# Values by head group with the first group moved into the image before, and a reordered opening of image 0, in a fused vision-transformer layer

## The chip, the cores and the metric

The kernel runs on one core of a Trainium2 chip. The metric is device time in microseconds (us) of one execution, taken as the median of several runs. The engines are PE (TensorE: matmuls, transposes, weight loads), DVE (VectorE), ACT (ScalarE), POOL (GpSimd) and SP (SyncE, which only issues transfers here). All run their own instruction streams in order and meet at semaphores.

## The reference

Eight images of 3 x 512 x 512 are cut into 1024 patches of 768 values each and go through one transformer layer with a mixture-of-experts feed-forward part. What matters here:

```
h = patches @ Wp + bp + (relu(xy @ W1 + b1) @ W2 + b2)       # 1024 x 256 for each image
a = layernorm(h)                                             # no gamma, beta
n = layernorm(a) * gamma + beta
q, k, v = split(n @ W_qkv.T)                                 # 8 heads of 32
gate = sigmoid(a @ W_gate.T + b_gate)
attn = softmax(q k^T / sqrt(32))                             # 1024 x 1024 for each head
out = (attn^T v) * gate                                      # weights indexed by query i, summed over i
h = h + a + out @ W_final.T + b_final
x = layernorm(h)
H = gelu(x @ W1 + b1);  probs = softmax(H @ Wg + bg)         # 1024 hidden, 8 experts
h = h + probs[argmax] * (H @ Wd[argmax] + bd[argmax])
```

All is float32 in and out.

## The kernel before

**Tiles.** An image is 1024 tokens, 8 tiles of 128 rows by 256 columns. `hres` holds h for two images in turn, `a` the first norm, `n` the second; `nt` and `at` are n (with gamma and beta) and a, transposed. `qk` holds q and k of one head group in a high and a low part, each [32 rows per head, 1024], and `stq`, `stk` hold these stacked three times in 96 rows (high/high, low/high, high/low), so that one matmul gives scores of full precision. `v` is [128, 8 tiles, 256], `vs` is v divided by the softmax sums, `pr` a ring of eight tiles of exponentials. PSUM (`ps`) has 8 banks of 512 columns: 0 to 3 take scores of two steps in turn, 4 and 5 the attention output, 6 and 7 (`spare`) everything else.

**Loops.** For each image b there are 64 steps k: two head groups of 32 steps (`G_STEPS`), each step one head and one tile of 128 queries. A step is `score` (PE, two matmuls of 512 columns), a maximum (DVE, `nmax`), an exponential with its sum (ACT), and, every fourth step, `scale_v` (DVE) and then `weigh` (PE). Score k waits for exponential k - 2. All else is put between the steps by hand-written tables (`QK1_AT`, `EMBED_AT`, `GATE_AT`, `TURN_AT`, `QK0_AT`, and `LOW*_AT`, `WEIGH_AT`). While image b runs its steps, PE also projects q and k of group 1 (steps 0 to 7), embeds image b + 1 (steps 8 to 31), and in the second half computes gates, transposes n and a of image b + 1 and projects q and k of its group 0 (steps 49 to 59). Step 32 holds the long insertion: `router(b - 1)` on PE and ACT (the hidden layer and the logits of the image before), and on DVE `norm_1(b + 1)` (statistics and a), `block_turn` (32 x 32 transposes of the hidden layer for the store), `stats_2`, the logit copies and `norm_2` (n). POOL computes each norm's reciprocal root (`root`: one addition, one power) and adds a and the final bias into `hres`.

**The seam between images.** After step 63 PE runs `values(b, 0)`, the last `weigh` of the image before, `values(b, 1)`, `final(b - 1)`, the gates of group 0 and then score 0. ACT reads v out of PSUM, DVE applies the gate, adds the result of `final` into `hres` and takes the statistics of the third norm. SP issues the 24 stacking transfers of group 0 once all scores of the image before are done, and score 0 waits for all 24.

**The opening.** PE computes the position term of all tiles first (K=3 matmul, relu, K=128 matmul, and a K=2 matmul that adds the bias), ACT copies it to `posb`, then PE embeds image 0 tile by tile through two buffers (`xt`), which SP refills. DVE and ACT, which split w_ffn1 into two parts, and PE wait for all 20 constants (`consts`) first. Then DVE and POOL do both norms, PE transposes and projects, and image 0 starts. After image 7 a router, a sort of all tokens by expert and the expert matmuls follow; nothing there is touched.

On PE the lines of the trace are: L430, L437 and L438 position, L448 embedding, L460 transposes of n and a, L469 q and k, L481 scores, L495 `weigh`, L509 values, L515 gates, L531 `final`, L544 transposes for the router, L552 to L554 hidden layer, L562 and L569 logits. On DVE L873 and L877 are statistics, L883 normalises, L910 makes the low part of q or k, L891 adds the embedding, L967 is `block_turn`, L1020 the maximum; on SP L287 and L289 are the stacking transfers.

## Time and profile before

| | |
|---|---|
| median of 3 runs | 1888.89 us (1886.69 to 1890.84) |
| the profiled execution | 1891.02 us, its span 1889.2 us |
| busy: PE, DVE, ACT, POOL | 1668.8, 1222.3, 946.8, 311.1 us |
| busy share of the span | 88%, 65%, 50%, 16% |
| first score | 114.27 us |
| first values matmul of images 0, 1, 2, 3 | 96.53, 254.27, 425.73, 599.02 us |
| stacking transfers | 2 x 192 of 128 KB, median 2.5 us from issue to landing |
| DMA, mean over the span; highest slice | 99 GB/s; 206 GB/s |

All times are from the start of the span. "Busy" of PE adds up overlapping instructions' stretches once; matmul ends are modelled. A row of the timeline merges neighbouring instructions of one kind. Its numbers are the start, the length, the engine, the line, what is written and read, the shape, the count, and in brackets the engine's idle time before it with what ended that. An fp32 matmul of the program is two PE instructions in the trace (x24 is 12 matmuls); a transpose is one.

### The profile page before, as it was taken

Reading aid. Unit: us, or ns where it says so; the run is one execution under the profiler, and the core shown is the slowest. Engines: PE = TensorE matmul, PEld = TensorE weight load, DVE = VectorE, ACT = ScalarE, POOL = GpSimd, SP = SyncE. Lnnn points to the kernel's source line nnn. Section 1 sums busy time; section 2 is a strip of 40 time slices with the busy share of each in tenths; the row PEclk is TensorE's granted clock in tenths of the full one; section 3 lists DMA queues with packets and bytes.
Section 4 is the critical chain, followed back from the end, with each engine's and each line's share of the span. In section 5 each row is a group of like instructions: output and inputs, shape, how many; then the busy total and the mean of one; then the engine's idle time right before and its main releaser. Section 6 shows DMA issues by size and latency. Waiting matters only on the chain.

```text
span 1889.2 us, 29246 instructions
## 1 busy us (share of the span) xinstructions
PE 1668.8 (88%) x10884; PEld 1128.4 (60%) x10884; DVE 1222.3 (65%) x2027; ACT 946.8 (50%) x1564; POOL 311.1 (16%) x239
## 2 busy tenths in 40 slices
PE   8587799989999999999899999999797715999998
PEld 4445456646655564566466555645353504999998
DVE  0347767776776887677767768776766487444443
ACT  1144656575665657565746656475655330222222
POOL 0200200200020011002000200200000072455553
PEclk9789899999999999999999999999898957999999
DMA  3133041704342252417044432513060391566663
GB/s 117 34 92 95 15 106 51 156 1 116 96 101 62 79 129 46 107 51 156 4 121 100 91 83 65 129 38 90 11 146 1 85 205 62 181 202 206 205 198 133
DMA packets 124151, 187.31 MB, mean 99 GB/s; under 512 B 14941, under 2 KB 89325, under 8 KB 123888
## 3 DMA queue, kind: packets, MB, share of 16 engines
q1 hardware_dynamic: 108016, 121.48, 27.5%
q0 software_dynamic: 16000, 63.98, 10.4%
q8 instruction: 91, 1.49, 0.3%
q14 instruction: 44, 0.36, 0.1%
HBM read 84.72 MB, written 51.38 MB: 72 GB/s over the span
## 4 chain that ended last, share of the span: by engine, by line
PE 66%; DVE 19%; issue 7%; ACT 4%; DMA 1%; POOL 1%; SPq 1%; POOLq 0%; DVEq 0%; ACTq 0%
PE ps L481 12%; PE ps L722 11%; PE ps L495 10%; PE ps L448 8%; DVE nmax L1020 6%; PE ps L469 3%; PE ps L710 3%; DVE bst L873 3%; ACT pr L819 3%; PE ps L531 3%; PE ps L509 3%; PE ps L552 2%; PE ps L554 2%; PE ps L553 2%; PE ps L515 2%
## 5 line engine op out<-in xcount | busy, mean ns | idle before, releaser
L1020 DVE TENSOR_REDUCE nmax<-ps 128x1 f32<-128x1024 f32 x512 | 624.0, 1221 | 228.4 <-PE ps L481 219.5
L819 ACT ACTIVATE pr<-ps,nmax 128x1024 f32<-128x1024 f32 x512 | 570.1, 1114 | 302.5 <-DVE nmax L1020 297.6
L481 PE MATMUL ps<-stk,stq 96*128 96x512 f32 x1024 | 411.5, 486 | 78.2 <-ACT pr L819 57.9
L481 PEld LDWEIGHTS ps<-stk,stq 96*128 96x128 f32 x1024 | 171.6, 195 | 278.8 <-ACT pr L819 167.1
L495 PE MATMUL ps<-pr,vs 128*32 128x256 f32 x4096 | 275.1, 390 | 16.2 <-DVE vs L922 16.2
L722 PE MATMUL ps<-wd,hg 128*128 x1728 | 225.4, 287 | 0.0
L343 POOL TENSOR_SCALAR vare<-mv 128x8 f32<-128x8 f32 x24 | 5.7, 238 | 1311.2 <-DVE mv L877 1311.2
L722 PEld LDWEIGHTS ps<-wd,hg 128*128 128x128 f32 x1728 | 212.7, 193 | 0.0
L495 PEld LDWEIGHTS ps<-pr,vs 128*32 128x32 f32 x4096 | 109.8, 110 | 165.5 <-issue 78.5
L853 ACT ACTIVATE hg<-ps 128x512 fp32r<-128x512 f32 x144 | 78.5, 597 | 240.6 <-PE ps L710 240.6
L448 PE MATMUL ps<-wp,xt 128*128 128x256 f32 x768 | 196.1, 382 | 2.2 <-DMA xt<-x_in 1.5
L448 PEld LDWEIGHTS ps<-wp,xt 128*128 128x128 f32 x768 | 145.5, 190 | 31.7 <-DMA xt<-x_in 2.7
L789 ACT ACTIVATE ht<-ps,bf 128x512 f32<-128x512 f32 x128 | 88.0, 688 | 139.9 <-PE ps L554 138.3
L469 PE MATMUL ps<-nt,wqk 128*128 128x512 f32 x256 | 133.0, 605 | 3.5 <-DVE qk L910 2.8
L1141 DVE TENSOR_TENSOR hg<-ps,hg 128x512 fp32r<-128x512 f32 x144 | 92.9, 685 | 49.6 <-ACT hg L853 49.5
L552 PE MATMUL ps<-nt_high,wf 128*128 128x512 f32 x256 | 105.3, 411 | 1.8 <-DVE nt_low L959 1.5
L1148 DVE SCALAR_TENSOR_TENSOR rows<-ps,slot_prob,rows 128x256 f32<-128x256 f32 x72 | 34.8, 483 | 111.0 <-PE ps L724 111.0
L554 PE MATMUL ps<-nt_high,wf 128*128 128x512 f32 x256 | 103.7, 405 | 0.0
L553 PE MATMUL ps<-nt_low,wf 128*128 128x512 f32 x256 | 102.6, 401 | 0.0
L819 ACT ACTIVATION_READ_ACCUMULATOR pr<-ps,nmax 128x1 f32 x512 | 99.5, 194 | 0.0
L408 POOL DMA_INDIRECT out<-rows,slot_to x72 | 72.3, 1004 | 125.0 <-DVE rows L1148 115.0
L710 PE MATMUL ps<-ident,rows 128*128 128x128 f32 x576 | 76.3, 277 | 7.2 <-DMA rows<-token_rows,slot_from 7.2
(122 smaller groups left out, 1811.0 us busy)
## 6 DMA issues: line engine op xcount, KB each, us to landing
xt<-x_in SPq DMA_DIRECT2D x64, 384.0 KB, 3.1
stq<-qk SPq DMA_DIRECT2D x192, 128.0 KB, 2.5
stk<-qk SPq DMA_DIRECT2D x192, 128.0 KB, 2.5
token_rows<-staged_b SPq DMA_DIRECT2D x64, 256.0 KB, 4.2
token_rows<-staged_a SPq DMA_DIRECT2D x64, 256.0 KB, 4.5
token_rows<-hres POOLq DMA_DIRECT2D x8, 1024.0 KB, 5.2
wd_raw<-w_down SPq DMA_DIRECT2D x64, 128.0 KB, 3.3
rows<-token_rows,slot_from POOLq DMA_INDIRECT x72, 4.7
```

Source lines behind the costliest of these rows:

```text
L448: last = mm(spare(t)[:, 0:D], xt[:, t % 2, k, :], wp[:, k, :], start=(k == 0), stop=(k == KC - 1))
L469: last = mm(spare(j), wqk[:, c, w * D + g * P:w * D + (g + 1) * P], nt[:, c, hf * HALF:(hf + 1) * HALF], start=(c == 0), stop=(c == DC - 1))
L481: last = mm(ps[:, 2 * (k % SR) + j, :], stq[:, hh, i * P:(i + 1) * P], stk[:, hh, j * 512:(j + 1) * 512], start=True, stop=True)
L495: last = mm(ps[32 * hh:32 * hh + 32, O_BANK + j // 2, (j % 2) * D:(j % 2 + 1) * D], vs[:, gi % 2, hh, :], pr[:, (4 * gi + hh) % PR, j * D: ...
L552: mm(spare(bank), w_high, nt_high[:, c, half], start=(c == 0), stop=False)
L553: mm(spare(bank), w_high, nt_low[:, c, half], start=False, stop=False)
L554: last = mm(spare(bank), w_low, nt_high[:, c, half], start=False, stop=(c == DC - 1))
L710: last = nc.tensor.transpose(ps[:, 2 * (s % 2) + c, q * P:(q + 1) * P], rows[:, s % RING, (4 * c + q) * P:(4 * c + q + 1) * P], ident[:])
L722: mm(o, hg[:, s % 2, h_part, k, :], wd[:, w_part, bass.ds(e, 1), k, :], start=(k == 0 and h_part == w_part), stop=False)
L819: actv(pr[:, k % PR, :], ps[:, 2 * (k % SR):2 * (k % SR) + 2, :].rearrange("p a n -> p (a n)"), ACT.Exp, bias=nmax[:, k % 16:k % 16 + 1], ...
L1020: V.reduce_max(nmax[:, k % 16:k % 16 + 1], ps[:, 2 * (k % SR):2 * (k % SR) + 2, :].rearrange("p a n -> p (a n)"), AX_X, negate=True).then_ ...
L1141: V.tensor_tensor(hg[:, s % 2, 1, 4 * c:4 * c + 4, :].rearrange("p k n -> p (k n)"), ps[:, 2 * (s % 2) + c, :], high_part.bitcast(F32), AL ...
```

## The change

1. **Values by head group.** `values(b, g, h)` computes the 128 columns of head group g for four tiles. It is 8 matmuls of 128 columns; before, a block was 4 matmuls of 256 columns. Group 0 of image b + 1 is computed in steps 61 and 63 of image b (`VALUE_AT`), and read by ACT there (`valued`); group 1 stays at the seam.
2. **Opening.** SP loads x of image 0 ahead of the constants, six tiles of it into the ring `pr`; w_patch, pos_w2 and the bias are issued by ACT, the bias broadcast to all partitions. PE embeds four tiles while ACT applies the relu, then alternates two position tiles with one embedding tile. The position term's bias is added by DVE. DVE takes each tile's statistics between the additions. The wait for the constants is split in two (`early`, `consts`), and the split of w_ffn1, now staged in the second half of `hres`, comes after the first values.
3. **One set of statistics for both norms.** With variance s of h, a's variance is s / (s + eps), so 1 / sqrt of (s + eps) and of (s (1 + eps) + eps^2) normalise h directly to a and to n. `stats_2` and one call of `root` go for each image. POOL does two additions and one power of 16 elements (before, twice one addition and a power of 8). n is normalised before a, both after the logit copies; the transposes of n and a wait for each separately; POOL's sum waits for a.
4. **Stacking.** One transfer moves the q and the k part of a row block: 12 of 256 KB for a group instead of 24 of 128 KB, with a semaphore for each head, and each of the first four scores waits for its head's three.

The diff, cut to its core:

```diff
+        st = tensor(sa, "st", [96, 2, 4, TOKENS], F32R)
+        stq, stk = st[:, 0], st[:, 1]
...
+        STACK = ((0, 3, 2), (1, 3, 1), (0, 4, 3))
...
+        VALUE_AT = {G_STEPS + 29: 0, G_STEPS + 31: 1}
...
+            for dst, src in ((posin, pos_in), (posw1, pos_w1)):
+                sp.dma_start(dst, src).then_inc(S["pos_in0"], 16)
+            for t in range(2):
+                sp.dma_start(xt[:, t], x[0, t]).then_inc(x_in[t], 16)
+            for t in range(2, TILES):
+                sp.dma_start(x_first[:, t - 2], x[0, t]).then_inc(S[f"x_first{t // 2 - 1}"], 16)
+            for dst, src in ((vecs[:, 0, :], ln_gamma), (vecs[:, 1, :], ln_beta), (vecs[:, 2, :], b_gate),
+                             (ident[:], identity), (wqk[:], w_qk), (wv[:], w_v), (wg[:], w_gate)):
+                sp.dma_start(dst, src).then_inc(S["early"], 16)
+            for dst, src in ((bfin[:], b_final), (wf1_in, w_ffn1), (wfin[:], w_final), (bf1[:], b_ffn1),
...
-                    for r in range(3):
-                        src = slice(32 * hh, 32 * hh + 32)
-                        dst = slice(32 * r, 32 * r + 32)
-                        sp.dma_start(stq[dst, hh, :].bitcast(F32), qk[src, 0, r % 2, :].bitcast(F32)
-                                     ).then_inc(stacked[g], 16)
-                        sp.dma_start(stk[dst, hh, :].bitcast(F32), qk[src, 1, r // 2, :].bitcast(F32)
-                                     ).then_inc(stacked[g], 16)
+                    src = slice(32 * hh, 32 * hh + 32)
+                    for r, (first, end, step) in enumerate(STACK):
+                        sp.dma_start(st[32 * r:32 * r + 32, :, hh, :].bitcast(F32),
+                                     qk_parts[src, first:end:step, :].bitcast(F32)).then_inc(stacked[g][hh], 16)
...
+            def root_1(b):
+
+                hold(pool, "var1", b + 1)
+                nc.gpsimd.tensor_scalar(vare[:, 0], mv[:, 0, :, 1], EPS, None, ALU.add).then_inc(S["eps1"], 1)
+                nc.gpsimd.tensor_scalar(vare[:, 1], mv[:, 0, :, 1], 1.0 + EPS, EPS * EPS, ALU.mult, ALU.add
+                                        ).then_inc(S["eps1"], 1)
+                wait(pool, "eps1", 2 * b + 2)
+                nc.gpsimd.tensor_tensor(rstd[:, 0:2], vare[:, 0:2], half_neg[:], ALU.pow).then_inc(S["rstd1"], 1)
...
+            def position(t):
+                o = ps[:, 4 + t // 2, (t % 2) * D:(t % 2 + 1) * D]
+                for c in range(DC):
+                    last = mm(o, posr[:, c, t * P:(t + 1) * P], posw2[:, c, :], start=(c == 0), stop=(c == DC - 1),
+                              skip_group_check=True)
+                last.then_inc(S["pos_mm2"], 1)
+
+            def first_embed(t):
+                if t < 2:
+                    wait(pe, x_in[t], 16)
+                elif t % 2 == 0:
+                    wait(pe, f"x_first{t // 2 - 1}", 32)
+                source = xt[:, t] if t < 2 else x_first[:, t - 2]
+                for k in range(KC):
+                    last = mm(ps[:, t // 2, (t % 2) * D:(t % 2 + 1) * D], source[:, k, :], wp[:, k, :],
+                              start=(k == 0), stop=(k == KC - 1), skip_group_check=True)
+                last.then_inc(S["emb_mm"], 1)
+
+            pe.wait_ge(S["pos_in0"], 16 * 2)
             for c in range(DC):
                 for hf in range(2):
-                    mm(ps[:, 2 * c + hf, :], posw1[:, c * P:(c + 1) * P], posin[:, hf * HALF:(hf + 1) * HALF],
+                    mm(ps[:, 4 + 2 * c + hf, :], posw1[:, c * P:(c + 1) * P], posin[:, hf * HALF:(hf + 1) * HALF],
                        start=True, stop=True).then_inc(S["pos_mm"], 1)
+            pe.wait_ge(S["wp_in"], 16)
+            for t in range(4):
+                first_embed(t)
+            pe.wait_ge(S["pos_in1"], 16 * 2)
             pe.wait_ge(S["pos_relu"], 4)
-            pe.wait_ge(S["setup"], 1)
-            for t in range(TILES):
-                o = ps[:, 4 + t // 2, (t % 2) * D:(t % 2 + 1) * D]
-                for c in range(DC):
-                    mm(o, posr[:, c, t * P:(t + 1) * P], posw2[:, c, :], start=(c == 0), stop=False, skip_group_check=True)
-                mm(o, ones[0:2, :].bitcast(F32), posbias, start=False, stop=True, skip_group_check=True).then_inc(S["pos_mm2"], 1)
-            pe.wait_ge(S["pos_done"], 4)
+            for t in range(4):
+                position(2 * t)
+                position(2 * t + 1)
+                first_embed(t + 4)
...
-                wait(pe, "n_ready", b + 1)
+                wait(pe, ("n_ready", "a_ready")[w // 2], b + 1)
...
-                if k % G_STEPS == 0:
-                    wait(pe, stacked[g], (b * 24 + 24) * 16)
+                if k % G_STEPS < 4:
+                    wait(pe, stacked[g][hh], (b + 1) * 3 * 16)
...
-            def values(b, pair):
-                if pair == 0:
-                    wait(pe, "qk_lo", b * 8 + 4)
-                for j in (2 * pair, 2 * pair + 1):
-                    if j >= 2:
-                        wait(pe, "v_read", b * 4 + j - 1)
-                    for t in range(2):
-                        for c in range(DC):
-                            last = mm(spare(j)[:, t * D:(t + 1) * D], nt[:, c, (2 * j + t) * P:(2 * j + t + 1) * P],
-                                      wv[:, c, :], start=(c == 0), stop=(c == DC - 1), skip_group_check=True)
-                    last.then_inc(S["v_mm"], 1)
+            def values(b, g, h):
+                if g == 0:
+                    wait(pe, "qk_lo", b * 8 + 3 + h)
+                else:
+                    wait(pe, "v_read", b * 4 + h + 1)
+                for t in range(4):
+                    for c in range(DC):
+                        last = mm(spare(h)[:, t * P:(t + 1) * P], nt[:, c, (4 * h + t) * P:(4 * h + t + 1) * P],
+                                  wv[:, c, g * P:(g + 1) * P], start=(c == 0), stop=(c == DC - 1),
+                                  skip_group_check=True)
+                last.then_inc(S["v_mm"], 1)
...
-                for t in range(TILES):
-                    for part in range(3):
-                        embed(b, t, part)
-                wait(pe, "emb_h", b * TILES + TILES)
+                wait(pe, "pos_done", 4)
                 for j in range(8):
                     turn(b, j)
                 wait(pe, "tr_read", b * 8 + 8)
                 for j in range(4):
                     for c in range(DC):
                         project(b, 0, j, c)
+                for h in range(2):
+                    values(b, 0, h)
+            pe.wait_ge(S["early"], 16 * N_EARLY)
+            front_start(0)
             pe.wait_ge(S["consts"], 16 * N_CONSTS)
-            front_start(0)
...
-                values(b, 0)
+                values(b, 1, 0)
                 if before:
                     for j in range(4):
                         weigh(b - 1, 15, j)
-                values(b, 1)
+                values(b, 1, 1)
...
+                    if after and k in VALUE_AT:
+                        values(b + 1, 0, VALUE_AT[k])
...
+            nc.scalar.dma_start(wp[:], w_patch).then_inc(S["wp_in"], 16)
+            nc.scalar.dma_start(posw2, pos_w2).then_inc(S["pos_in1"], 16)
+            nc.scalar.dma_start(posbias, pos_bias[None, :, :].broadcast_to([P, 2, D])).then_inc(S["pos_in1"], 16)
...
+            def valued(b, g, h):
+                wait(act, "v_mm", b * 4 + 2 * g + h + 1)
+                wait(act, "vs_ready", b * 16 - 8 * (1 - g))
+                actv(v[:, 4 * h:4 * h + 4, g * P:(g + 1) * P], spare(h).rearrange("p (t d) -> p t d", t=4), ACT.Identity,
+                     scale=0.5).then_inc(S["v_read"], 1)
...
-            def stats_2(b):
-                wait(dve, "a_ready", b + 1)
-                stats(a, b, 2)
-            def norm_2(b, before):
+            def norm_2(b, par, before):
                 if before:
                     wait(dve, "xt_mm", b * 4 - 4)
-                normalise(n, a, b, 2, "n_ready")
+                normalise(n, hres[:, par], b, 2, "n_ready")
+                normalise(a, hres[:, par], b, 1, "a_ready")
...
+                if t % 2 == 0:
+                    wait(dve, "pos_mm2", t + 2)
+                    V.tensor_tensor(posb[:, t:t + 2, :], ps[:, 4 + t // 2, :].rearrange("p (t d) -> p t d", t=2),
+                                    posbias[:, 0, None, :].broadcast_to([P, 2, D]), ALU.add).then_inc(S["pos_done"], 1)
+                    wait(dve, "pos_done", t // 2 + 1)
                 embedded(0, 0, t)
-            norm_1(0, 0)
-            stats_2(0)
-            norm_2(0, False)
+                if t >= 1:
+                    wait(dve, "emb_h", t)
+                    V.bn_stats(bst[:, 0, t - 1, :], hres[:, 0, t - 1, :])
+            wait(dve, "emb_h", TILES)
+            V.bn_stats(bst[:, 0, TILES - 1, :], hres[:, 0, TILES - 1, :]).then_inc(S["stats1"], 1)
+            aggregate(0, 1)
+            norm_2(0, 0, False)
             for j in range(4):
                 low(0, 0, j)
+            dve.wait_ge(S["wf1_high"], 1)
+            V.tensor_tensor(wf1[:, 1], wf1_in, wf1[:, 0].bitcast(F32), ALU.subtract).then_inc(S["setup"], 1)
...
-                        if after:
-                            stats_2(b + 1)
...
-                            norm_2(b + 1, before)
+                            norm_2(b + 1, 1 - par, before)
```

**PE, the opening** (after the branch, before that of the first rows; `wp` is w_patch, `pr` after the change also holds x):

```order
L437 MATMUL ps<-at,nt 128x256 x2
L438 MATMUL ps<-at,ones 128x256
L448 MATMUL ps<-wp,xt 128x256 x48
L460 MATMUL ps<-ident,n 128x128 x8
```

That was before, where the first two rows stand eight times. Now:

```order
L450 MATMUL ps<-wp,xt 128x256 x12
L450 MATMUL ps<-wp,pr 128x256 x12
L439 MATMUL ps<-at,nt 128x256 x4
L450 MATMUL ps<-wp,pr 128x256 x6
L439 MATMUL ps<-at,nt 128x256 x4
```

The K=2 matmuls (L438) are gone; half of the embedding stands first, and the other half alternates with the position tiles.

**PE, from step 61 of image 0 to score 0 of image 1**, before:

```order
L481 MATMUL ps<-stk,stq 128x512 x4
L495 MATMUL ps<-pr,vs 32x256 x8
L481 MATMUL ps<-stk,stq 128x512 x4
L495 MATMUL ps<-pr,vs 32x256 x8
L509 MATMUL ps<-wv,nt 128x256 x8
L495 MATMUL ps<-pr,vs 32x256 x16
L509 MATMUL ps<-wv,nt 128x256 x8
L531 MATMUL ps<-wfin,gate 128x256 x16
```

and now:

```order
L509 MATMUL ps<-st 128x512 x4
L536 MATMUL ps<-wv,nt 128x128 x8
L523 MATMUL ps<-pr,vs 32x256 x8
L509 MATMUL ps<-st 128x512 x4
L536 MATMUL ps<-wv,nt 128x128 x8
L523 MATMUL ps<-pr,vs 32x256 x8
L536 MATMUL ps<-wv,nt 128x128 x8
L523 MATMUL ps<-pr,vs 32x256 x16
L536 MATMUL ps<-wv,nt 128x128 x8
L559 MATMUL ps<-wfin,gate 128x256 x16
```

Two of four blocks of values now stand between score 61 and score 62, and behind score 63, each ahead of a `weigh`.

**DVE, at step 32 of image 1**, before:

```order
L873 BN_STATS bst<-hres 128x6 x8
L877 BN_AGGR mv<-bst 128x2 x8
L883 TENSOR_SCALAR a<-hres,mv,rstd 128x256 x8
L967 STREAM_TRANSPOSE staged_b<-ht 128x16x32 x4
L873 BN_STATS bst<-a 128x6 x8
L877 BN_AGGR mv<-bst 128x2 x8
L967 STREAM_TRANSPOSE staged_a<-ht 128x16x32 x4
L974 COPY xt<-ps 128x512
L978 COPY logits<-ps 128x32
L883 TENSOR_SCALAR n<-a,mv,rstd 128x256 x8
```

and now:

```order
L908 BN_STATS bst<-hres 128x6 x8
L915 BN_AGGR mv<-bst 128x2 x8
L1002 STREAM_TRANSPOSE staged_b<-ht 128x16x32 x4
L1002 STREAM_TRANSPOSE staged_a<-ht 128x16x32 x4
L1009 COPY xt<-ps 128x512
L1013 COPY logits<-ps 128x32
L921 TENSOR_SCALAR n<-hres,mv,rstd 128x256 x8
L921 TENSOR_SCALAR a<-hres,mv,rstd 128x256 x8
```

The second statistics are gone and a has moved behind the logit copies.

## Rows read from the trace of the kernel before

**Rows 1.** The page, the chain of work that ended last, share by engine.

```profile
PE 66%; DVE 19%; issue 7%; ACT 4%; DMA 1%; POOL 1%; SPq 1%; POOLq 0%; DVEq 0%; ACTq 0%
```

**Rows 2.** Timeline, opening (start, length, engine, what, count, idle before).

```profile
4.24 7.19 PE L430 MATMUL ps<-pr 3*128 3x512 f32 x8 [4.24 <-DMA at<-pos_bias]
...
12.12 2.08 PE L437 MATMUL ps<-at,nt 128*128 128x256 f32 x4 [0.69 <-ACT nt L742]
...
38.10 6.90 PE L448 MATMUL ps<-wp,xt 128*128 128x256 f32 x24 [0.69 <-ACT posb L745]
39.96 2.29 DVE L868 TENSOR_TENSOR wf<-a,wf 128x2048 fp32r<-128x2048 f32 x1 [24.13 <-ACT wf L749]
...
57.38 5.45 PE L448 MATMUL ps<-wp,xt 128*128 128x256 f32 x24 [0.53 <-DMA xt<-x_in]
```

**Rows 3.** Busy us by stretch: PE, PEld, DVE, ACT, POOL, granted clock, DMA, GB/s.

```profile
12.00:38.00 26.00, 25.30 (x48) 13.39 (x48) 0.17 (x1) 2.40 (x6) 0.00 (x0) 1.00 0.16 52
...
528.00:540.00 12.00, 12.00 (x47) 9.58 (x47) 8.67 (x18) 4.47 (x7) 8.86 (x2) 0.86 0.69 138
701.00:713.00 12.00, 12.00 (x59) 9.15 (x62) 9.38 (x20) 5.72 (x8) 8.57 (x2) 1.00 0.77 152
```

**Rows 4.** Timeline, the norms of image 0 and the transposes.

```profile
66.07 0.64 DVE L877 BATCH_NORM_AGGREGATE mv<-bst 128x2 f32<-128x6 f32 x8
66.89 0.24 POOL L343 TENSOR_SCALAR vare<-mv 128x8 f32<-128x8 f32 x1 [66.04 <-DVE mv L877]
67.23 1.67 POOL L346 TENSOR_TENSOR rstd<-vare,half_neg 128x8 f32<-128x8 f32 x1
...
77.15 2.67 DVE L883 TENSOR_SCALAR n<-a,mv,rstd 128x256 f32<-128x256 f32 x8 [2.12 <-POOL rstd L346]
...
82.02 1.94 PE L460 MATMUL ps<-ident,a 128*128 128x128 f32 x8
```

**Rows 5.** Timeline, from the last low part to the first score.

```profile
95.78 0.69 DVE L910 SCALAR_TENSOR_TENSOR qk<-ps,qk 128x512 fp32r<-128x512 f32 x1 [1.03 <-ACT qk L769]
...
96.53 7.17 PE L509 MATMUL ps<-wv,nt 128*128 128x256 f32 x32 [1.41 <-DVE qk L910]
...
103.54 3.60 PE L515 MATMUL ps<-at,wg 128*128 128x512 f32 x8
...
111.51 0.59 SPq L289 DMA_DIRECT2D stk<-qk  x1
...
114.27 1.22 PE L481 MATMUL ps<-stk,stq 96*128 96x512 f32 x2 [7.13 <-DMA stk<-qk]
```

**Rows 6.** Timeline of DVE, middle of image 0.

```profile
178.22 2.70 DVE L873 BATCH_NORM_STATS2 bst<-hres 128x6 f32<-128x256 f32 x8
...
195.71 2.35 DVE L1020 TENSOR_REDUCE nmax<-ps 128x1 f32<-128x1024 f32 x2
```

**Rows 7.** Timeline of PE, seam between images 2 and 3.

```profile
594.98 1.07 PE L495 MATMUL ps<-pr,vs 128*32 128x256 f32 x16 [0.65 <-DVE vs L922]
...
597.35 0.73 PE L481 MATMUL ps<-stk,stq 96*128 96x512 f32 x2 [0.64 <-ACT pr L819]
...
599.02 3.72 PE L509 MATMUL ps<-wv,nt 128*128 128x256 f32 x16
...
618.03 1.04 PE L481 MATMUL ps<-stk,stq 96*128 96x512 f32 x2
```

**Rows 8.** Timeline of DVE and PE, middle of image 2.

```profile
520.76 2.67 DVE L873 BATCH_NORM_STATS2 bst<-a 128x6 f32<-128x256 f32 x8
...
527.11 1.06 PE L569 MATMUL ps<-pick,xt 128*128 128x8 f32 x8 [0.95 <-DVE xt L974]
...
541.01 2.32 DVE L1020 TENSOR_REDUCE nmax<-ps 128x1 f32<-128x1024 f32 x2
```

**Rows 9.** Timeline of PE, transposes for the router in image 2.

```profile
506.54 1.97 PE L544 MATMUL ps<-ident,n 128*128 128x128 f32 x16
```

**Rows 10.** Line L509: length of one in ns, least, median, most.

```profile
L509 PEld LDWEIGHTS ps<-wv,nt x256: 185/190/191, 96.5 to 1297.2; 128*128 128x128 f32 x128
```

115 lines of the change are left out of this document (53 added, 62 removed).

## The prediction

> **What bounds the kernel now.** I read the chain of waits first: two thirds of it is PE, a fifth DVE [rows 1]. That share is a mean over stages, so I then read the timeline engine by engine for four places that the change touches: the opening of image 0, the middle of image 0 (step 32), the middle of a later image, and the seam between two images. What is to be seen:
>
> - Opening. PE computes the position term, then embeds, then waits 17 us for two layer norms, then projects, then waits for the stacking DMAs. The first score starts at 114.27 [rows 5]. PE is busy 25.30 of the 26 us from 12 to 38 and its granted clock is recorded as 1.00 [rows 3], yet four instructions of 256 columns take 2.08 us there, and in the last third of the embedding 24 of the same shape take 5.45 [rows 2]: 0.50 against 0.227 us each, the pace of 1.2 against 2.4 GHz. The change of pace lies inside the first 24 embedding instructions (6.90 us).
> - Middle of image 0. No router runs there, and DVE alone carries it: 178.22 to 195.71, from the statistics of image 1 to the first maximum of the second head group [rows 6].
> - Middle of a later image. PE idles 0.95 us before the small logit transposes, since DVE was late [rows 8].
> - Seam. From 599.02 PE runs without a gap to the first score at 618.03 [rows 7], and DVE goes from the statistics of the last layer norm straight into the first maximum. Before that, in the last three score steps, PE idles 0.65 us (waiting for the scaled v) and 0.64 us (waiting for the exponentials) [rows 7].
>
> From about 175 on the middle part of each image (steps 8 to 31) is PE throughout and is not touched; the tail after image 7 is not touched either.
>
> **The opening, term by term.** After the change PE starts once the first two small loads have landed. Before, it waited for four and started at 4.24; I take 3.6 (no more than 4.24 in any case). The 4 matmuls of K=3 keep their 7.19 us [rows 2]: 10.8. Then come 96 embedding instructions and 32 for the position term without the K=2 matmuls (those 8 leave PE). The first 12 embedding instructions, in which the pace changed, took 6.90 less 12 x 0.227, about 4.2 us; the other 116 at 0.227 take 26.3: PE ends at 41.3. If the position matmuls stay at 0.50, it is 32 x 0.27 = 8.7 more; if none of it ever gets fast, 128 x 0.50 = 64, so 75. I take the fast pace, since the same kind of instruction (128 rows, 256 columns) had it in the embedding [rows 2] and no K=2 matmul stands between them any more. The loads: w_patch, pos_w2 and the bias move to ACT's queue and x goes ahead of the constants. At the 384 KB of one x tile it is 4.3 MB in all by 25 us, when PE wants the last tiles, 172 GB/s, which the page's busy slices reach; so I cost the reordering at nothing; the cover is the 7.19 us of K=3 matmuls for w_patch, and a late w_patch costs its lateness one for one.
>
> DVE's per-tile statistics now run between the embeddings; the last two adds, two statistics and the 0.64 us of aggregation end 2.4 us after PE: 43.7, against 66.71 before [rows 4]. **Gain 23.0.**
>
> From there to n: before 66.71 to 79.82, 13.1 us (two rounds of statistics, POOL, normalise). After: two additions of 0.24 instead of one, one power, one normalise of 2.67 [rows 4]. The power now has 16 elements instead of 8; nothing in the trace shows that size. Bounds: 1.67 (no dearer) and 3.34 (twice); I take 3.3, because a row of 8 elements at 1.67 against an addition at 0.24 is work per element. 0.2 + 0.24 + 0.24 + 0.1 + 3.3 + 0.1 + 2.7 = 6.9. **Gain 6.2** (7.9 at the low bound). a is now normalised after n, and the third group of transposes, which began 2.2 us after n was done [rows 4], can begin 2.7 after: **loss 0.5.**
>
> From the last low part (ends 96.47) to the first score (114.27): 17.8 us, set by 24 issues on SP, the last at 111.51 and landing 2.7 later; PE's values and gates were done by 107.1 [rows 5]. Now the score needs the first 3 of 12 DMAs. Each carries twice the bytes. Bounds for one issue: 0.59 [rows 5] and 1.2 (twice). At the high bound the first three land 3.6 + 2.7 = 6.3 us in and the last of 12 at 17.1; the fourth score is wanted some 7 us after the first, at about 16.6, so even this costs half a microsecond, and at 0.59 nothing. PE becomes the limit: values begin 1.4 us before the last low part is done (PE waited that long for it [rows 5], and the first block now needs three parts only), then 7.6 us of values (a run is costed below) and 3.45 of gates: 9.7. **Gain 8.1.** The split of w_ffn1 moves in here, on ACT between two reads of v and on DVE before the first maximum (2.29 us [rows 2]), both while PE works on values and gates for 9.7 us; if that cover fails it costs what is left over, at most the 2.29.
>
> Opening in sum: 23.0 + 6.2 - 0.5 + 8.1 = 36.8, so the first score at about 77.5. PE no longer idles 7.13 us before it [rows 5], and the first scores then ran at half pace (1.22 us for what takes 0.73 later [rows 5, 7]): 1 us more. **37.8.**
>
> **Middle of image 0.** Of the 17.5 us between 178.22 and 195.71 [rows 6], the second statistics (2.71 + 0.64) and a POOL round of 2.1 us go, and 0.24 + 1.65 for the larger power come: **gain 3.5** (5.2 if the power costs 1.67). Score 32 wants its three DMAs at about 180, so what is late next is still DVE.
>
> **Middle of images 1 to 6.** Without the second statistics (2.67 + 0.64 [rows 8]) DVE follows the GELUs and has the logit sums before PE asks: the 0.95 us go, and with them about 0.3 of the wait in PE's queue. But n and a are now both normalised after this point, 2.67 us more on DVE before the turns of the second half. From the small transposes to the first maximum it was 13.90 us here [rows 8], with a mean clock of 0.86 over the twelve from 528 [rows 3]; that is 3.4 us at half, which costs 1.6. In the next image the same stretch has 1.00 (the row from 701), so some 12.3; I take the two to alternate. Laid end to end DVE now needs 1.3 + 5.35 + 1.2 + 8 x 0.6 = 12.7 us from there. So the gain is 1.25 where PE's dip stays, and 0.8 where DVE becomes the limit; both bounds: 0 and 2.1 (dip gone). **6 x 1.0 = 6.0.** Image 7 normalises nothing, gain 0.
>
> **Seam, seven times.** All of v for one image is 32 PE instructions of 256 columns in two runs of 3.72 us [rows 7]. After: four runs of 16 instructions of 128 columns. Nearest rows for such a run: 16 transposes with 128 columns and a full weight load, 1.97 us to the end of the last [rows 9]; 8 instructions with full fp32 weight loads and hardly any columns, 1.06 us [rows 8], or 0.13 each. So 1.9 a run: v costs what it cost. Two runs leave the seam (3.7 us) and enter steps 61 and 63, where PE idled 1.29 us, which is all they can hide in. Going through the steps: score 62 starts 1.2 us later, score 63 0.5 later, the last weighing and final each 1.2 earlier. ACT's two reads of 0.6 us stand behind exponentials 61 and 63 while ACT waits for DVE anyway. As final moves, so do DVE's adds, statistics and the first maximum. Bounds 0.3 and 1.4; **7 x 1.2 = 8.4.** The 12 stacking DMAs have some 23 us there, from the end of score 63 to the fourth score of the next image (618.03 and some 4 us more), so they cost nothing up to 1.7 us each.
>
> The Trainium skill speaks against this cut. Its page "TensorE: Matmul & The Clock Gate", section "Back-to-back issue gap", says that with a weight load for each matmul the spacing at 128 columns is above what the columns alone give (about 81 ns instead of 56). As an estimate from that page, 1.45 times the half of 0.227 would be 0.165 us an instruction, and the sum about 24 us worse. Rows 8 and 9 show 0.12 to 0.13, and I go by them.
>
> **Sum.** 37.8 + 3.5 + 6.0 + 8.4 = 55.7. The profiled execution took 1891.02 us, so 1835.3; it was 2.13 us over the median of the runs shown, so 1833.2 in their terms.
>
> **Rivals.**
> 1. The slow clock stays. PE was busy from 12 to 38 and still at the 1.2 GHz pace [rows 2, 3], so position and embedding together may not wake it. Against it: the embedding did. If all of it is slow, PE ends at 75 instead of 41.3: 34 us of the opening's gain are lost, 1867. (The Trainium skill, same page, section "What's actually happening", has sustained activity release the clock; the stretch from 12 to 38 does not agree with it as it stands.)
> 2. Only the opening pays. The seam and the later middles give nothing, because PE's filled idle time pushes the last scores and the exponentials by as much, and DVE's later n and a take the rest: 14.4 less, 1848.
> 3. Weight loads surface at 128 columns. A load of this kind is 0.19 us long [rows 10]; if the loads set the pace with their full length, a run costs 3.05, which is 1.15 more, four times in eight images: 37, so 1870. Against it: the 1.06 and the 1.97 us [rows 8, 9].
> 4. Slower: the merged stacking DMA is much dearer to issue. It reads two strided rows per partition into a strided tile; no row shows that form. Per DMA of c us, each seam loses 12 (c - 1.7) and the opening 12 (c - 1.16); the 55.7 us are gone at c = 2.2. At 2.4, four times today's 0.59, it is 74 us: 1907.
> 5. Better than summed: the power costs no more than now in both places (3.4), and the dips go: 1826.
> That the change doesn't do what it says is excluded by the order of the instructions.
>
> **How the numbers follow.** Forecast 0.55 (1833, own range 1824 to 1844, the upper end being the slow position matmuls), rival 1 0.12, rival 2 0.15, rival 3 0.06, rival 4 0.03, rival 5 0.07, near zero for some reason unseen 0.02. The range must reach rivals 2 and 5 and may leave out 1, 3 and 4, 0.21 in all: 1822 to 1850. Within 0.2% (3.8 us, what can be told from no change here) 0.01; slower 0.03; faster 0.96.
>
> **What would show it.** In the changed profile: first score near 77.5; embedding and position instructions at 0.227 us from about 15 on; the power at 3.3; step 32 of image 0 about 14 us after its first statistics; no PE idle time before the small transposes of images 1 to 6; runs of values of 1.9 us; final 1.2 us nearer to score 61. Wrong would be a pace of 0.50 beyond 20 us, values over 2.2 us a run, an issue above 1.2 us, or DVE later than PE at the seam for another reason than the statistics.

## The result and the profile after

The changed kernel takes 1824.16 us (median of 4 runs, 1823.65 to 1824.39) against 1889.07 us for the kernel before beside it (4 runs, 1886.69 to 1890.84): ratio 0.9657, 95% interval 0.964 to 0.9674. That is 64.9 us gained; 55.7 were forecast. The result lies within the forecast's range of 1822 to 1850, 9 us below its 1833. The profiled execution took 1824.39 us, 66.6 less than that of before, and the account below is made against that.

Lines have moved: L450 and L476 embed, L439 is the position term, L509 scores, L523 weighs, L536 computes values, L559 is the final projection, L597 the small logit transposes, L1066 the maximum, L296 the stacking DMAs.

The chain of work that ended last, and busy time of each engine; the chain has hardly changed in kind against [rows 1]:

```profile
PE 1631.2 (90%) x11124; PEld 1125.0 (62%) x11124; DVE 1201.0 (66%) x1904; ACT 943.0 (52%) x1560; POOL 307.8 (17%) x231
...
PE 68%; DVE 18%; issue 7%; ACT 5%; DMA 1%; SPq 1%; POOL 0%; POOLq 0%; DVEq 0%; ACTq 0%
```

The timeline of the opening, to be laid beside [rows 2, 4, 5] (start, length, engine, what, count, idle before it):

```profile
5.30 7.19 PE L457 MATMUL ps<-pr 3*128 3x512 f32 x8 [5.30 <-DMA pr<-pos_w]
12.42 8.13 PE L450 MATMUL ps<-wp,xt 128*128 128x256 f32 x24
20.39 5.34 PE L450 MATMUL ps<-wp,pr 128*128 128x256 f32 x24
25.57 1.89 PE L439 MATMUL ps<-at,nt 128*128 128x256 f32 x8
...
44.88 0.64 DVE L915 BATCH_NORM_AGGREGATE mv<-bst 128x2 f32<-128x6 f32 x8
...
46.35 2.94 POOL L350 TENSOR_TENSOR rstd<-vare,half_neg 128x16 f32<-128x16 f32 x1
...
49.32 2.67 DVE L921 TENSOR_SCALAR n<-hres,mv,rstd 128x256 f32<-128x256 f32 x8 [3.80 <-POOL rstd L350]
...
54.63 1.97 PE L488 MATMUL ps<-ident,a 128*128 128x128 f32 x8 [0.55 <-DVE a L921]
...
67.71 7.31 PE L536 MATMUL ps<-wv,nt 128*128 128x128 f32 x64
...
69.26 14.15 SPq L296 DMA_DIRECT2D st<-qk  x12
...
77.89 1.04 PE L509 MATMUL ps<-st 96*128 96x512 f32 x2
...
83.21 0.73 PE L509 MATMUL ps<-st 96*128 96x512 f32 x2 [2.09 <-DMA st<-qk]
...
87.28 1.22 PE L509 MATMUL ps<-st 96*128 96x512 f32 x2 [2.48 <-DMA st<-qk]
...
87.34 0.60 ACT L797 ACTIVATE qk<-ps 128x512 fp32r<-128x512 f32 x1 [4.57 <-DMA st<-qk]
```

What is to be seen: the first score starts at 77.89, against 114.27 before [rows 5] and 77.5 forecast. Then two scores wait 2.09 and 2.48 us for a stacking DMA each, and ACT waits 4.57 us for the last of them before it overwrites qk. The last score of the fence took 1.22 us instead of 0.73: PE came out of the wait at half its pace, as it had in [rows 5].

The values by line: length of one in ns (least, median, most), of the matmuls and of their weight loads:

```profile
L536 PE MATMUL ps<-wv,nt x512: 272/275/377, 67.7 to 1236.3; 128*128 128x128 f32 x171
...
L536 PEld LDWEIGHTS ps<-wv,nt x512: 186/192/193, 67.6 to 1236.2; 128*128 128x128 f32 x171
```

The page's row on the stacking DMAs (KB each, us from issue to landing):

```profile
st<-qk SPq DMA_DIRECT2D x192, 256.0 KB, 5.1
```

The seam between images 2 and 3, against [rows 7]:

```profile
549.98 0.73 PE L509 MATMUL ps<-st 96*128 96x512 f32 x2 [0.35 <-ACT pr L854]
...
550.54 1.95 PE L536 MATMUL ps<-wv,nt 128*128 128x128 f32 x16
...
552.42 1.07 PE L523 MATMUL ps<-pr,vs 128*32 128x256 f32 x16
...
554.46 1.95 PE L536 MATMUL ps<-wv,nt 128*128 128x128 f32 x16
...
563.07 7.07 PE L559 MATMUL ps<-wfin,gate 128*128 128x256 f32 x32
```

And three stretches as busy us of PE, PEld, DVE, ACT, POOL, granted clock, DMA share, GB/s: of image 1 from the router's transposes to the maximum of step 32 (the "middle"), then from there to its final projection, and the latter again for image 2 (the "second half"):

```profile
297.51:329.31 31.80, 30.99 (x184) 22.93 (x184) 23.83 (x59) 15.73 (x24) 9.22 (x5) 1.00 0.73 171
...
329.31:393.70 64.39, 59.52 (x460) 32.92 (x453) 45.73 (x57) 47.27 (x82) 3.35 (x1) 1.00 0.22 51
...
497.34:563.07 65.73, 60.89 (x460) 33.74 (x453) 45.82 (x57) 47.39 (x82) 3.35 (x1) 0.97 0.21 50
```

The same two second halves before, images 1 and 2:

```profile
367.98:434.80 66.82, 60.86 (x429) 32.18 (x421) 45.81 (x57) 47.54 (x82) 0.92 (x1) 0.97 0.20 44
...
541.01:608.09 67.08, 61.08 (x429) 32.12 (x421) 45.91 (x57) 47.65 (x82) 0.00 (x0) 0.97 0.21 44
```

The last four show what the forecast had not looked at. A second half comes in two lengths, 64.39 with a clock of 1.00 and about 65.73 with 0.97. Of images 0 to 6, all seven had a fall of the clock before; after, only images 0, 2 and 5 do. I cut both traces at the same events (a middle of image 0 runs from the first embedding of image 1 to the maximum of step 32); the account in us, before less after:

| part | forecast | measured | |
|---|---|---|---|
| opening, to the first embedding of image 1 | 37.8 | 31.6 | 131.23 to 99.60 |
| middle of image 0 | 3.5 | 4.1 | 64.48 to 60.37 |
| middles of images 1 to 6, at clock 1.00 | 6.0 | 6.8 | 32.94 to 31.80 |
| seven seams, at the same clock | 8.4 | 9.3 | 67.06 to 65.73 |
| clock falls that are gone, and image 7 and the tail | 0 | 14.7 | below |
| sum | 55.7 | 66.5 | 66.6 |

The 14.7: three middles of before, at a clock of 0.95, took 34.47 instead of 32.94, and no such fall is left (4.6); four second halves (images 1, 3, 4 and 6) lost theirs, at 1.3 or so each (5.2); image 7 gave 3.9 and the tail 1.5; the final-to-embedding stretches gave -0.4. Each trace is one execution. The opening of the changed kernel came to 99.60 in this one and to 98.15 in another below, and the opening of before, with the same instructions, to 131.23, 131.92 and 132.50, so this pair of traces gives the opening the least of what these would (31.6 to 34.4). Image 7 and the tail differ by as much among versions that don't touch them: the tail is 427.6 here, 429.2 in the run with 24 transfers and 429.6 in the one with the stacking by halves. Their 5.4 us can't be put down to the change.

### The profile page after: what moved, and what is told of

Its sections match the earlier page's. It is cut to its first block, busy times and chain, and to the rows that moved or that the text cites. A ratio compares the mean times of both kernels' runs of the same rounds, so it can differ in the third digit from the quotient of the medians.

```text
span 1822.6 us, 29454 instructions
## 1 busy us (share of the span) xinstructions
PE 1631.2 (90%) x11124; PEld 1125.0 (62%) x11124; DVE 1201.0 (66%) x1904; ACT 943.0 (52%) x1560; POOL 307.8 (17%) x231
## 4 chain that ended last, share of the span: by engine, by line
PE 68%; DVE 18%; issue 7%; ACT 5%; DMA 1%; SPq 1%; POOL 0%; POOLq 0%; DVEq 0%; ACTq 0%
PE ps L509 12%; PE ps L752 11%; PE ps L523 11%; PE ps L476 8%; DVE nmax L1066 6%; ACT pr L854 3%; PE ps L740 3%; PE ps L559 3%; PE ps L536 3%; PE ps L497 3%; PE ps L580 2%; PE ps L582 2%; PE ps L581 2%; PE ps L543 1%; PE ps L450 1%
## 5 line engine op out<-in xcount | busy, mean ns | idle before, releaser
L1066 DVE TENSOR_REDUCE nmax<-ps 128x1 f32<-128x1024 f32 x512 | 623.7, 1221 | 216.7 <-PE ps L509 209.8
L509 PE MATMUL ps<-st 96*128 96x512 f32 x1024 | 399.6, 474 | 70.5 <-ACT pr L854 60.8
L509 PEld LDWEIGHTS ps<-st 96*128 96x128 f32 x1024 | 168.2, 191 | 266.5 <-ACT pr L854 128.6
L523 PE MATMUL ps<-pr,vs 128*32 128x256 f32 x4096 | 271.7, 386 | 11.5 <-DVE vs L957 11.5
L523 PEld LDWEIGHTS ps<-pr,vs 128*32 128x32 f32 x4096 | 108.8, 109 | 153.4 <-issue 70.4
L476 PE MATMUL ps<-wp,xt 128*128 128x256 f32 x672 | 172.8, 378 | 0.0
L476 PEld LDWEIGHTS ps<-wp,xt 128*128 128x128 f32 x672 | 126.3, 189 | 25.2 <-DVE qk L945 1.2
```

What stands on the lines that cost most here:

```text
L476: last = mm(spare(t)[:, 0:D], xt[:, t % 2, k, :], wp[:, k, :], start=(k == 0), stop=(k == KC - 1))
L509: last = mm(ps[:, 2 * (k % SR) + j, :], stq[:, hh, i * P:(i + 1) * P], stk[:, hh, j * 512:(j + 1) * 512], start=True, stop=True)
L523: last = mm(ps[32 * hh:32 * hh + 32, O_BANK + j // 2, (j % 2) * D:(j % 2 + 1) * D], vs[:, gi % 2, hh, :], pr[:, (4 * gi + hh) % PR, j * D: ...
L1066: V.reduce_max(nmax[:, k % 16:k % 16 + 1], ps[:, 2 * (k % SR):2 * (k % SR) + 2, :].rearrange("p a n -> p (a n)"), AX_X, negate=True).then_ ...
```

## The experiments

Two things are to be explained: why the opening gave 6 us less than summed, and where 15 us came from that nobody had counted. My theory on the first is that the stacking DMAs are limited by the rate at which bytes move, with SP's issue time following from it; the rivals are the form of the merged DMA and SP's queue. On the second it is that short PE waits beside the small router matmuls let the clock fall; the rivals are that a term of the sum was simply worth more, or that something else shortened these stretches. The first four runs take the parts of the change back. "Beside it" is the kernel before, run on the same chip together with the changed one.

### The values back at the seam

```diff
-        VALUE_AT = {G_STEPS + 29: 0, G_STEPS + 31: 1}
+        VALUE_AT = {}
...
-                for h in range(2):
-                    values(b, 0, h)
...
-                values(b, 1, 0)
+                values(b, 0)
...
-                values(b, 1, 1)
+                values(b, 1)
```

values() and ACT's four reads of v are those of before.

> The changed kernel with the values as before the change: four blocks of 256 columns, all at the seam. Theory A (the seam gives 1.35 us for the move itself, and the rest of the 2.1 us a seam that the trace shows is PE's clock, which no longer falls): plus 7 x 1.35 = 9.5 us, 1833.6, and the clock falls as seldom as in the changed kernel. Theory B (the move gives all 2.1 us): plus 14.5, 1838.7.

Measured: 1835.13 us (1834.04 to 1837.48), beside it 1888.27; ratio 0.971 [0.9681, 0.9739]. So the cut of v is worth 11 us by the medians; the profiled execution, 1837.48, is the slowest of its four, and its span is 13.1 above that of the changed kernel. Image 2, middle's end to final:

```profile
500.95:568.01 67.06, 60.97 (x428) 32.25 (x421) 45.88 (x57) 47.58 (x82) 3.36 (x1) 0.97 0.23 54
```

The seven second halves of images 0 to 6 take 66.99 to 67.11 with a clock of 0.94 to 0.97; the middles stay at 31.78. Against 65.73 in the changed kernel, also with a fall, the move itself gives 1.33 a seam, 9.3 in all. The rest of the 13.1 is that four images got their fall back (4 x 1.35 = 5.4), and the short form of image 7's first half (66.43 against 67.60) gave 1.2 the other way. So theory A had the price of the move right, and its claim that the clock would fall as seldom as in the changed kernel was wrong. The fall comes some 5 us after step 32, where this kernel issues the same instructions as the changed one.

### Two statistics and two powers again

```diff
-                stats(hres[:, par], b, 1)
+                stats(hres[:, par], b, 1)
+                normalise(a, hres[:, par], b, 1, "a_ready")
...
+                        if after:
+                            stats_2(b + 1)
...
-                root_1(b)
+                root(1, b)
+                root(2, b)
```

n is normalised from a, as before; POOL does a power of 8 elements twice.

> The changed kernel with the second statistics and the second round of POOL put back, in the opening and for every image. Both theories: 6 us in the opening and 4 in the middle of image 0. For the six later middles theory A expects 1.15 us each and, because PE then idles 0.95 us again, the clock to fall again in some of them (1.5 us each time): 1841 to 1846. Theory B expects 1.15 us each and no change of the clock: 1841.

Measured: 1845.5 us (1841.52 to 1846.21), ratio 0.976 [0.9729, 0.979]: 21 us slower than the changed kernel. By place: opening 5.4, middle of image 0 4.1, middles of images 1 to 6 6.6 (32.90 against 31.80), the rest in the second halves (images 1 to 4 have a fall here, 2 and 5 in the changed kernel), image 7 and the tail. The middle of image 2, and in PE's timeline the small transposes in it:

```profile
477.18:510.08 32.90, 31.07 (x184) 22.81 (x184) 26.61 (x75) 15.73 (x24) 12.11 (x6) 1.00 0.79 183
```

```profile
497.76 1.06 PE L597 MATMUL ps<-pick,xt 128*128 128x8 f32 x8 [1.02 <-DVE xt L1013]
```

The 1.02 us of PE idle time before the small transposes is back, as in [rows 8], and so is the length of 32.9, but the clock stays at 1.00, where before three of six middles had 34.47. So the wait alone isn't enough for a fall, and its going is not shown to be why the middles lost theirs.

### Twenty-four stacking transfers

```diff
-                        sp.dma_start(st[32 * r:32 * r + 32, :, hh, :].bitcast(F32),
-                                     qk_parts[src, first:end:step, :].bitcast(F32)).then_inc(stacked[g][hh], 16)
+                        dst = slice(32 * r, 32 * r + 32)
+                        sp.dma_start(stq[dst, hh, :].bitcast(F32), qk[src, 0, r % 2, :].bitcast(F32)
+                                     ).then_inc(stacked[g][hh], 16)
+                        sp.dma_start(stk[dst, hh, :].bitcast(F32), qk[src, 1, r // 2, :].bitcast(F32)
+                                     ).then_inc(stacked[g][hh], 16)
```

> The changed kernel with the stacking as 24 transfers of 128 KB instead of 12 of 256 KB, still with a semaphore for each head. Theory A (the stacking is bound by bytes, some 170 GB/s): scores 1 to 3 of image 0 wait as long as now, 1824, within 1 us. Theory B (the merged form is what costs 1.18 us an issue and 5 us a landing): the waits of some 5 us go, 1819.

Measured: 1824.34 us (1822.97 to 1828.64), ratio 0.9658 [0.9625, 0.969]: no difference. The scores and ACT wait all the same:

```profile
85.72 1.22 PE L512 MATMUL ps<-st 96*128 96x512 f32 x2 [2.38 <-DMA st<-qk]
...
85.78 0.60 ACT L800 ACTIVATE qk<-ps 128x512 fp32r<-128x512 f32 x1 [4.05 <-DMA st<-qk]
```

SP issues 24 DMAs from 68.24 on, at 0.59 us and more each; the last issue begins at about 83.7. The 12 merged DMAs take 1.18 each to issue on the average (14.15 / 12) and land after 5.1, these cost half and land after 2.4. In the changed kernel the first three of the twelve were issued in 0.76, 0.59 and 0.75, with little under way, and the others in 1.11 to 1.40. So the merged form alone is no dearer to issue; the issue gets long once transfers are under way. The form of the DMA is not what the scores wait for. With 24 DMAs, 128 KB every 0.64 us is itself some 205 GB/s, so this run alone can't tell SP's own pace from a limit on the bytes; the 12 larger ones and the two queues below can.

### The opening alone

The three edits above together, and score 0 waits for all four heads, so that the new opening is left of the change: the embedding ahead, the order of the loads, the bias and the per-tile statistics on DVE, and the later split of w_ffn1.

```diff
                 if k % G_STEPS == 0:
                     for h4 in range(4):
                         wait(pe, stacked[g][h4], (b + 1) * 6 * 16)
```

> The new opening alone: values at the seam, two statistics, 24 transfers and one wait for all 24 as before the change. The embedding ends 18.8 us earlier than before the change and the per-tile statistics save 3 more, the rest of the chain to the first score is the old one: first score near 92, total 1889 less 22 = 1867, and less still by what the clock gives at random (up to 5 us).

Measured: 1869.55 us (1858.18 to 1870.74), ratio 0.9874 [0.9832, 0.9916]. The first score starts at 92.96 (92 expected). The opening is 21.1 shorter than before (110.16 to the first embedding of image 1), and the whole span 20.5. The falls are back in the middles too, four of them at 34.45, though neither the values at the seam alone nor the two statistics alone brought one back there. The second half of image 2:

```profile
520.12:587.23 67.11, 61.12 (x428) 32.17 (x421) 45.90 (x57) 47.69 (x82) 0.00 (x0) 0.97 0.17 40
```

### The waits of before filled

Two matmuls with 512 columns, into a bank that is overwritten afterwards, in each of two places where PE waits: ahead of the small transposes [rows 8], and behind the second half's logit matmuls, ahead of the score of step 33 that waits 1.09 us for ACT.

```diff
                 hidden(b, 1, 0, 1)
+                if b < IMAGES - 1:
+                    for _ in range(2):
+                        mm(ps[:, 0, :], wg[:, 0, 0:P], at[:, 0, 0:HALF], start=True, stop=True)
...
                         partial_logits(b - 1, 1, 0)
+                        for _ in range(2):
+                            mm(spare(1), wg[:, 0, 0:P], at[:, 0, 0:HALF], start=True, stop=True)
```

> The kernel before with two matmuls more that nobody reads (fp32, 512 columns, 0.85 us) at two places of each later image where PE waits 0.95 to 1.1 us anyway: ahead of the small logit transposes, and behind the partial logits of the second half. Theory A (these waits let the clock fall, which costs 1.5 us three times in the middle and 1.3 us at most seams): the falls go, 1889 less about 12 = 1877. Theory B (the clock falls for another reason, or costs nothing there): 1889 or slightly more.

Measured: 1886.02 us (1882.85 to 1890.44), beside it 1890.09; ratio 0.9975 [0.9965, 0.9985]. Image 2, middle and second half:

```profile
507.03:540.46 33.43, 32.62 (x188) 23.60 (x188) 26.62 (x75) 15.71 (x24) 12.13 (x6) 1.00 0.84 176
...
540.46:606.74 66.28, 61.33 (x432) 32.12 (x425) 45.82 (x57) 47.54 (x82) 0.92 (x1) 1.00 0.21 47
```

In images 1 to 6 every fall is gone (clock 1.00 in all middles and second halves), yet the kernel gains only 4 us. The two took 1.7 us together, twice what I had taken, so that each pair sticks out of its wait by 0.5 (33.43 against 32.94), 6 us in all. Image 7 gets the filling too and has no such wait ahead of the small transposes: its middle takes 33.85 instead of 32.28, and its second half 62.12 instead of 60.40. Filling did what the theory says in images 1 to 6, and my filling was too large.

### The same behind the logits, in the changed kernel

```diff
                         partial_logits(b - 1, 1, 0)
+                        for _ in range(2):
+                            mm(spare(1), wg[:, 0, 0:P], at[:, 0, 0:HALF], start=True, stop=True)
```

> The changed kernel with two such matmuls behind the partial logits of the second half, where PE waits 1.18 us. Theory A: the two remaining falls of the clock behind step 32 (images 2 and 5, 1.34 us each) go, 1821.5. Theory B: 1824.

Measured: 1828.52 us (1826.44 to 1830.47), ratio 0.9678 [0.9662, 0.9694]: 4 us slower than the changed kernel by this, with intervals that overlap, and neither theory's time. Image 2, then the second half of image 7:

```profile
496.70:561.56 64.86, 61.19 (x464) 33.71 (x457) 45.73 (x57) 47.25 (x82) 3.33 (x1) 1.00 0.21 50
...
1335.25:1397.38 62.13, 47.70 (x352) 20.24 (x344) 43.52 (x53) 39.97 (x67) 0.00 (x0) 0.95 0.07 18
```

Here too the falls of images 2 and 5 are gone, and the second halves of images 1 to 6 have 64.86 to 64.89, which is 0.47 more than the 64.39 without a fall; too large again. Over the six images the two effects cancel (389.2 us against 389.0), so the loss isn't there. What the profiled execution shows of it is in image 7: 62.13 with a clock of 0.95, where the changed kernel has 58.73 and 1.00. A filling that frees six images is no promise for the seventh.

### The changed kernel started later

Four matmuls ahead of the first embedding, which wait for the first tile of x, and nothing else.

```diff
+            wait(pe, x_in[0], 16)
+            for _ in range(4):
+                mm(ps[:, 0, 0:D], xt[:, 0, 0, :], wp[:, 0, :], start=True, stop=True, skip_group_check=True)
             for t in range(4):
                 first_embed(t)
```

> The changed kernel with four matmuls more that nobody reads (256 columns) ahead of the first embedding, which delays all that follows by 2 to 3 us. If the clock falls by what PE does around step 32 alone: plus 2 to 3 us, 1827, the same two falls. If it depends on where in time these places lie: the falls move to other images and their number changes, anything from 1823 to 1836.

Measured: 1827.86 us (1827.26 to 1828.74), ratio 0.9671 [0.9655, 0.9688]. The opening is 1.35 longer, the total 3.7 (3.4 in the profiled execution, of which 2.7 lie in image 7). Images 2 and 4; image 3 has 64.39 and a clock of 1.00:

```profile
498.25:563.97 65.72, 60.86 (x460) 33.74 (x453) 45.83 (x57) 47.32 (x82) 3.32 (x1) 0.97 0.21 50
...
835.62:901.37 65.75, 60.92 (x460) 33.75 (x453) 45.82 (x57) 47.35 (x82) 3.33 (x1) 0.97 0.21 50
```

The falls are now in images 2 and 4 instead of 2 and 5, with the same instructions in each. So the wait and the instructions around it do not alone decide which image is hit. That it is the place in time is not shown: in the changed kernel's other execution (first embedding of image 1 at 98.15) and with the stacking on two queues (at 102.57), on either side of this run's 100.95, the falls are in images 2 and 5.

### Stacking on two queues

For the first group of image 0 SP issues heads 0 and 1, POOL heads 2 and 3.

```diff
-                for hh in range(4):
+                for hh in range(4 if b or g else 2):
...
+            pool.wait_ge(S["qk_lo"], 4)
+            for hh in (2, 3):
+                for r, (first, end, step) in enumerate(STACK):
+                    nc.gpsimd.dma_start(...).then_inc(S[f"first{hh}"], 16)
```

> The changed kernel with the stacking of heads 2 and 3 of image 0's first group issued by POOL's queue beside SP's. Theory A (one queue moves 170 GB/s at most in this form, two move more): the waits before scores 2 and 3 (2.1 and 2.5 us) shrink, 1820. Theory B (the bytes share one limit): heads 0 and 1 come later as much as 2 and 3 earlier, 1824 to 1826.

Measured: 1825.72 us (1824.78 to 1832.86), ratio 0.9669 [0.9647, 0.9692]: nothing gained, and the opening is 3 us longer. The first score:

```profile
69.11 9.85 SPq L296 DMA_DIRECT2D st<-qk  x6
...
69.40 3.46 POOL L378 DMA_DIRECT2D st<-qk  x6 [5.79 <-DVE qk L957]
...
82.11 0.95 PE L518 MATMUL ps<-st 96*128 96x512 f32 x2 [3.80 <-DMA st<-qk]
```

```profile
st<-qk POOLq DMA_DIRECT2D x6, 256.0 KB, 8.2
```

POOL issues its six in 3.46 us, but they take 8.2 to land, and SP's own six now need 9.85 to issue, 1.64 each. The two queues share what the one had. It is the bytes, and heads 2 and 3 now take them from head 0, which is wanted first: its third transfer lands at 82.06, after 11.5 us, and the first score starts at 82.11 instead of 77.89.

### Stacking by halves

What is left is to start earlier. The first half of the columns has its low parts before the second half has, so for the first group of image 0:

```diff
+                if b == 0 and g == 0:
+                    for half in range(2):
+                        cols = slice(half * HALF, (half + 1) * HALF)
+                        sp.wait_ge(S["qk_lo"], 2 * half + 2)
+                        for hh in range(4):
+                            ...  # the three transfers of this head, columns cols
```

> The changed kernel; only in image 0 and its first head group the stacking goes in 24 transfers of half the tokens, and those of the first half start once the first two low parts are written, 3.4 us before the last. In the changed kernel the transfers run at 210 GB/s with the DMA engines busy 0.97 of the time, and ACT waits 4.6 us for the last of them before it may overwrite qk. If the bytes set that end: all are in 3.4 us earlier, 1824.2 - 3.4 = 1820.8, the first embedding of image 1 at 95 to 96. If the order of issue or the number of transfers matters more: no gain or a loss, 1824 to 1826.

> The changed kernel as it is, on the chip of the three beside it, to compare with: 1824, and the clock falling as before at images 2 and 5 behind step 32.

Measured: 1821.37 us (1820.93 to 1823.92), ratio 0.9636 [0.9603, 0.967], and 1822.26 us (1820.71 to 1829.4), ratio 0.9651 [0.9611, 0.9691], for the changed kernel again beside it. The opening of the former:

```profile
65.67 16.58 SPq L297 DMA_DIRECT2D st<-qk  x24
...
78.37 0.73 PE L519 MATMUL ps<-st 96*128 96x512 f32 x2
...
80.35 0.73 PE L519 MATMUL ps<-st 96*128 96x512 f32 x2 [0.39 <-DMA st<-qk]
...
84.25 0.73 PE L519 MATMUL ps<-st 96*128 96x512 f32 x2 [0.50 <-DMA st<-qk]
...
84.31 0.60 ACT L807 ACTIVATE qk<-ps 128x512 fp32r<-128x512 f32 x1 [0.72 <-DMA st<-qk]
```

SP starts at 65.67 instead of 69.26; the waits shrink from 2.09 and 2.48 to at most 0.50, ACT's from 4.57 to 0.72, and the scores that wait take 0.73, not 1.22. The first embedding of image 1 starts at 94.71, against 98.15 in the changed kernel beside it. From the first score on it is 16.34 us to there, against 21.26 beside it and 16.96 before: all that the stacking had cost behind the first score is back, and 1.5 of it is given back ahead of that score, 0.8 of them in the first embeddings (8.13 against 7.29). Of the 3.4 us the medians show 0.9, less than their spread. The falls lie elsewhere in this kernel, but are two as well (images 3 and 6). What takes the gain back in the profiled execution is the second half of image 0 (66.34 against 65.56), image 7 (1.9 more) and the tail (2.1 more), none of which the edit touches.

### One matmul instead of two

The same fillings with range(1): behind the logits in the kernel with the halves, and at both places in the kernel before.

```diff
                         partial_logits(b - 1, 1, 0)
+                        for _ in range(1):
+                            mm(spare(1), wg[:, 0, 0:P], at[:, 0, 0:HALF], start=True, stop=True)
```

> The stacking by halves, and one matmul more that nobody reads (0.85 us, within the 1.18 us that PE waits behind the partial logits of the second half; two of them, which took 1.7 us, cost 0.47 an image). If filling the wait keeps the clock up and costs nothing: every seam segment from step 32 to final at 64.4, two falls of 1.34 us less, 1818. If one is too little: falls in some images as now, 1821.

> The kernel before with one such matmul instead of two at each of the two places. If the clock's falls cost what the segments show (1.5 us three times in the middle, 1.3 us at seven seams) and one matmul prevents them at no cost: 1889 less 13 = 1876. If one is too little: 1889; in between if only some go.

Measured: 1815.58 us (1814.59 to 1816.51), ratio 0.9607 [0.9573, 0.964], and 1876.56 us (1875.34 to 1881.3), ratio 0.9932 [0.9904, 0.996]. Image 2 of the first, second half; then of the second, middle and second half:

```profile
491.85:556.21 64.36, 60.56 (x462) 33.23 (x455) 45.72 (x57) 47.29 (x82) 3.37 (x1) 1.00 0.21 51
```

```profile
505.31:538.24 32.93, 32.04 (x186) 23.15 (x186) 26.61 (x74) 15.71 (x24) 12.14 (x6) 1.00 0.84 179
...
538.24:604.00 65.76, 60.80 (x431) 31.58 (x423) 45.81 (x57) 47.53 (x82) 0.92 (x1) 1.00 0.21 47
```

One matmul of 0.85 us fits into the wait and costs nothing: 64.36 and 32.93 are the lengths without a fall (of a second half of before no such length is known, since all had one). In the kernel before, the middles of images 1 to 6 now take 32.93 and the second halves of images 1 to 6 65.72 to 65.76, where they took 32.9 or 34.47 and 66.78 to 67.08. Adding 14 matmuls whose result nobody reads makes the kernel before 12 us faster. In the changed kernel with the halves, 7 of them take the second halves of images 1 to 6 to 64.35 to 64.39, and that kernel is 6.7 us faster than the changed one beside it, the fastest of all here; by its profile 4.4 of that is the opening and 2.7 the two falls.

## Why the prediction was right, point by point

**Start and embedding, 23.0 forecast.** The statistics are complete at 45.52 (44.88 + 0.64), against 66.71: 21.2, and 21.1 in the run with the opening alone. The pace was right (24 embedding instructions in 5.34, 8 position instructions in 1.89, some 0.23 us each). What was off is the start: 5.30, where I had put 3.6 and "no more than 4.24 in any case". The two small loads landed 1.06 us later than the four had; why, no run here tested.

**Norms, 6.2 less 0.5.** From 45.52 to the end of n at 51.99 it takes 6.5, against 13.1: 6.6. The power over 16 elements took 2.94, nearer to the upper bound of 3.34 than to 1.67, against 3.3 taken. The transposes of a start at 54.63, 2.64 after n: the 0.5 was right.

**From the low part to the first score, 8.1.** What is left of 114.27 less 77.89 is 9.0. Values take 7.31 for 64 instructions of 128 columns.

**After the first score, 1.0 forecast.** This is the step that failed. I had written that the fourth score is wanted some 7 us after the first and that even the high bound for one issue, 1.2, costs half a microsecond. The issue took 1.18, the high bound, but the landing is 5.1 us and not 2.7, and neither is a constant: the first DMA, with nothing else of its kind under way, was issued in 0.76 and landed after 3.4. Both are what the rate at which the bytes move makes of them. The 12 transfers carry 3 MB; from the first issue to the last landing it took about 18 us in either form (96.50 to 114.2 before, 69.26 to 87.2 after), some 175 GB/s of stacking over the whole, and 210 of all transfers in this stretch:

```profile
76.00:84.00 8.00, 5.91 (x17) 2.94 (x16) 2.68 (x4) 3.79 (x6) 0.00 (x0) 1.00 0.97 210
```

The DMA share of 0.97 says it: the engines are full. I had split the cost into issue and landing and doubled the first alone. And the sum looked at score 3 only; ACT needs all twelve landed before it may overwrite qk, and it waited 4.57. With PE's half pace after its two waits, the first score's gain of 36.4 had become 31.6 at the first embedding of image 1. The three forms of stacking (24 transfers, two queues, halves) bear this out: only starting earlier helped, and with it the 21.7 us from the first score to the first embedding of image 1 became 16.3, where the forecast, 1.0 less than the 16.96 of before, asks for 16.0. So nearly the whole miss behind the first score is the stacking.

**Middles, 3.5 and 6.0.** 4.1 in image 0, where the smaller price of the power gives 0.4 of the 0.6; 1.14 instead of 1.0 in images 1 to 6, at the same clock. PE no longer idles before the small transposes there (0.95 before), and with the second statistics put back both the wait (0.99 to 1.03) and the 32.9 us return. My bounds of 0.8 and 1.25 hold it; which of the two engines sets those 31.80 us I did not separate.

**Seams, 8.4.** 1.33 instead of 1.2 each, shown by taking the move back. A run of 16 values took 1.95 (1.9 taken). From score 61 (549.98 in the fence above) to the final projection it is 13.09 us, against 14.49 before.

**The clock, not forecast but in rival 5.** I had alternating dips in the middles of the trace before in hand (0.86 in [rows 3]) and gave them 1.6 us each, in one bound. That they also sat in every second half, and that the change might free them, I had not looked up: windows over whole halves would have shown 0.97 in images 1 to 6. With image 7 and the tail it is the largest error of the forecast, +14.7, and hides the 6.2 lost in the opening. That the total came out 9 us from the forecast and inside its range is in part luck: two errors of opposite sign, neither foreseen.

**The rivals.** The slow clock did not stay: its pace ended within the first 24 embedding instructions. "Only the opening pays" is excluded by the run with the values at the seam (11 us) and the one with two statistics (21 us). Loads do not surface at 128 columns: 16 instructions in 1.95 us are 0.122 each, with weight loads of 192 ns beside them. The Trainium skill, page "TensorE: Matmul & The Clock Gate", section "Back-to-back issue gap", expects a penalty there for a weight load with each matmul; the measured cost is half that of 256 columns (0.227), so for these fp32 instructions the trace doesn't agree, and by the estimate of 0.165 the sum would have come out 24 us worse than forecast, on the wrong side of the result. The merged DMA's issue of 1.18 stays under the 1.7 from which the seams would have paid for it. Rival 5 was half right: all falls in the middles went, but the power was dearer. Its 1826 is close to the result without its mechanism. Why the middles lost their falls is not shown: each part put back alone brought none of them back, the three together did.

One reading of the prediction has to be set right. For 12 to 38 us [rows 3] print a granted clock of 1.00, and the prediction sets that against a pace of 0.50. The trace of before has no entry of the clock ahead of 41.08, nor that of the changed kernel ahead of 17.89, and the view prints 1.00 where it has none. The pace is the only witness there, and the first entry, at 2.4 GHz, falls within the first 24 embedding instructions in both, just where the pace changes.

**What is shown of the falls and what isn't.** Shown: with a matmul in those waits no fall is left in images 1 to 6 of either kernel, and with one of 0.85 us the middles of before and the second halves of the changed kernel have just the length that they have without a fall. Whether it is the wait that has to go, or whether a matmul more anywhere near it would do, no run tells: none was put elsewhere. (Image 0 runs without a router beside it, has a clock of 0.93 to 0.95 in its second half in every version, and was not taken apart; nor were image 7 and the tail.) Shown as well: the wait is not sufficient. The kernel with the two statistics has a wait of 0.99 to 1.03 in the middles of images 1 to 6 and no fall there; the changed kernel has the wait of 1.18 after step 32 in image 1 as in image 2, and a fall only in the latter; and in the kernel that started later one fall sits in another image. Why the values at the seam bring it back in all of images 1 to 6, with the same instructions around step 32, stays open.

## What to carry to other kernels

Cut the trace of before into whole stages and read each stage's clock before summing: two lengths of one stage with equal instructions are a fall, and a change elsewhere can free a stage of one or bring one back, here 10 us of 65 in images 0 to 6. Where PE waits about a microsecond next to light matmuls, try one spare matmul that fits inside the wait, and not a larger one, and look at the stages that have no such wait. Price a batch of DMAs by its bytes over the rate at which such a batch landed, not by issue plus one landing: merging or spreading them changed nothing here, and only starting them earlier did.

## What the runs showed of the hardware

- The granted clock fell after some of the PE waits of about 1 us next to the small matmuls of the logits; a fall cost 1.3 to 1.5 us. In the kernel before, image 2, the score that follows the logits waited, and the stretch from 544 had 0.78:

```profile
543.50 0.74 PE L481 MATMUL ps<-stk,stq 96*128 96x512 f32 x2 [1.09 <-ACT pr L819]
```

```profile
544.00:548.00 4.00, 3.96 (x16) 2.50 (x16) 2.55 (x3) 2.87 (x6) 0.00 (x0) 0.78 0.82 174
```

- In the changed kernel the same score waits 1.18 us in image 1 as in image 2; some 4 us on, two gate matmuls take 1.02 in image 1 and 1.90 in image 2:

```profile
331.88 0.70 PE L509 MATMUL ps<-st 96*128 96x512 f32 x2 [1.18 <-ACT pr L854]
...
335.71 1.02 PE L543 MATMUL ps<-at,wg 128*128 128x512 f32 x2
```

```profile
499.91 0.70 PE L509 MATMUL ps<-st 96*128 96x512 f32 x2 [1.18 <-ACT pr L854]
...
504.24 1.90 PE L543 MATMUL ps<-at,wg 128*128 128x512 f32 x2
```

- Busy as it was (25.30 of 26 us from 12 to 38 in the kernel before, position matmuls with 2 and with 128 rows), PE stayed at the pace of 1.2 GHz there. In the changed kernel the first 24 embedding instructions took 8.13 us and the next 24 5.34; in its other execution the first 24 took 7.29.
- Transfers within the core's memory, from 32 partitions to 32 others, moved 3 MB in about 18 us, some 175 GB/s, alike as 12 of 256 KB on one queue, as 24 of 128 KB, and on two queues. The issue time of a DMA of 256 KB on SP rose with what was under way, from 0.59 to 1.3 us on one queue and to 1.64 on the average beside POOL's.
- A power on POOL took 1.67 us for 8 elements a partition and 2.94 for 16: by these two, some 0.4 to start and 0.16 for each as an estimate.
